# Fused Swin block and conv mixer: dilated convolutions spread over four column tiles, and VectorE's order rewritten

## The chip, the cores and the metric

One core of one Trainium2 chip runs the whole program. The metric is the device time of one execution in microseconds (us); lower is better. The kernel before was run three times: 1600.66, 1603.93 and 1605.35 us, median 1603.93. The engines are called PE (TensorE, matrix products), DVE (VectorE), ACT (ScalarE), POOL (GpSimd) and SP (SyncE, which issues the DMAs).

## The reference

Sixteen images of 128 channels and 32 x 32 pixels (1024 tokens), all float32, pass through two layers. The first is a Swin block (window attention over 8 x 8 windows with 8 heads, then an MLP of width 512); its output is the input of the second, a mixer of convolutions:

```python
out0 = gelu(conv1x1(x))
h_out, v_out = 3x3(7 taps, dilation 11, along w), 3x3(the same along h)   # depthwise
feats = [conv2d(out0, pyr_w[i], pyr_b[i], pad=(d, d), dil=(d, d), groups=dim // 4)
         for i, d in enumerate((1, 6, 12, 20))]      # 32 channels each: the pyramid
pyr = 3x3 depthwise(fuse_w * concat(feats) + fuse_b)
x_sca = |ifft2(conv1x1(x) * fft2(conv1x1(x)) * mask)| ...    # spectral branch
out = relu(x + c0*(1+edge)*h_out + c1*(1+edge)*v_out + c2*(1-0.3*edge)*pyr + c3*point + c4*x_sca)
return conv1x1(out)
```

The weights c0 to c4 come from a softmax over a small gate that reads the mean of out0; edge is the sigmoid of a 3x3 convolution to one channel.

## The kernel before

The work of two images is interleaved. `both(n, i, f, late)` exists once for each engine and is the body of a hardware loop: it runs the mixer of image n beside the attention and MLP of image i = n+1, the first norm and the q, k, v products of image f = n+2, and the end of the mixer of image late = n-1. It runs 15 times (n = 0 to 14, 13 of them in the loop); a setup and the attention of image 0 stand before it, and `conv_only(15)` behind it. Every engine executes its own list in the order in which it is written, and waits on semaphores.

**PE.** The head: scores(i,0), in_conv (1x1, line 652), scores(i,1), edge_products, then parts of the pyramid between gap_products (659) and mid_products (665), two tiny products whose answers DVE turns into the gate. Then eight slots j, one for each pair of windows: conv_early(j), scores(i,j+2) (line 530, which writes bank 2 and so waits for DVE to have read the scores before), prob_transposes(j), conv_late(j), values(i,j) (553, into banks 1 and 3 in turn). conv_early and conv_late are hand-placed pieces of the mixer: the spectral branch's transforms (dft_rows, r_even, ..., last_even), x2_conv, and parts of the pyramid in slots 0 and 1; out_conv(late) stands in slot 0. Behind the slots: last_odd, project, pyramid_conv(0) (683), n2_transposes(0) (481), pyramid_conv(1), n2_transposes(1), and mlp (593, 603), with the q, k, v products of image f inside it.

**The pyramid** (`pyramid(n, k, steps)`, line 693). Dilation d has a [128 x 32] weight for each of its nine taps and writes partitions 32d to 32d+31 of PSUM, that is, it runs in column tile d of PE. Half k (16 rows) has bank 4+k. A part runs over some of the nine taps, and in each over the dilations 3, 2, 1, 0; each matmul has only the rows and columns for which the shifted pixel lies in the image, so tile 0 (dilation 1) has nearly whole matmuls and tile 3 (dilation 20) small ones. In float32 each is two matmul instructions. Parts: half 0 in the head (taps 0-1, 2-5, 6-8), half 1 in slot 0 (0-3) and slot 1 (4-8). ACT copies each half to `pyr` (pyr_copy, 1578); SP stacks it with 12 DMAs into `pyr_stack` (stack_pyramid, 426), which pyramid_conv reads.

**DVE.** The head: gate_axes and add_magnitude of the late image, bias_max(i,0), gap, bias_max(i,1), attention_vectors, mixture(late), scaled_input, even_part, route_logits. bias_max(i,j) (1008) adds the bias (which frees bank 2), takes the row maximum and subtracts it. Slots: scale_values(j-1) (1022: reciprocal and product), bias_max(j+2), and pieces of the mixer (conv_slot, 1222). The 3x3 taps of h_out and v_out are 17 instructions over `hv` (1144), placed by `SLOT_TAPS`: one in slot 6, one behind norm2(i,0), two behind norm1_stats(f,1), the other 13 at the end. The next iteration's gate_axes follows the last tap.

**ACT** has the Gelus, exponentials and most copies from PSUM; first_tap (1562) in slot 2 starts hv; n2_copy(i,0) stands between square_odd and deviation2(i,1). **POOL** computes the dilated row and column convolutions (axis_conv) from the moment `act` is there.

Of the kernel before, what the change touches and what calls it, by code (L numbers as in the profile page):

```python
# [27 lines left out]
ALU = mybir.AluOpType  # L28
# [5 lines left out]
P = 128  # L34
# [13 lines left out]
GRID1 = S1 * S1  # L48
AXIS_DIL, AXIS_TAPS = 11, 7
# [5 lines left out]
def layout(*entries):  # L55
# [11 lines left out]
    ("fuse_w", 1), ("fuse_b", 1), ("pyr_b", 1), ("vis_b", 1),  # L67
# [72 lines left out]
def swin_conv_kernel(nc, x, cols, rows, mats, cons, rel_index, out):  # L140
    with ExitStack() as ctx:
# [33 lines left out]
        fuse_bias = sb("fuse_bias", 1)  # L175
        proj_shift = sb("proj_shift", P)
# [34 lines left out]
        hv, py = sb("hv", SIDE, SIDE), sb("py", SIDE, SIDE)  # L211
        pyr_stack = sb("pyr_stack", 4, GRID1)
# [110 lines left out]
        pyr_ps = sem("pyr_ps")  # L323
# [62 lines left out]
        SLOT_TAPS = (1, 1, 1, 1, 1, 1, 1, 2, 2, 3, 5)  # L386
# [3 lines left out]
        def _(sp):  # L390
# [35 lines left out]
            def stack_pyramid(n):  # L426
                sp.wait_ge(pyr_sb, 2 * n + 2)
                for s in range(3):
                    for j in range(4):
                        src = pyr[32 * j:32 * j + 32].rearrange("p h w -> p (h w)")  # L430
                        sp.dma_start(pyr_stack[32 * s:32 * s + 32, j, 0:33 * S1 + SIDE], src[:, s:s + 33 * S1 + SIDE])\
                          .then_inc(pyr_stacked, 16)
# [43 lines left out]
        def _(pe):  # L476
# [200 lines left out]
            def pyramid_conv(n, k):  # L677
                pe.wait_ge(pyr_stacked, 16 * 12 * n + 16 * 12)
# [10 lines left out]
            def inside(first, count, off):  # L689

                return max(first, -off), min(first + count, SIDE - off)

            def pyramid(n, k, steps):

                pe.wait_ge(act_sb, 2 * n + 2)
                grids = bank[4 + k].rearrange("p (h w) -> p h w", w=SIDE)
                for step in steps:
                    t = PYR_ORDER[step]
                    for d, dil in reversed(tuple(enumerate(DILS))):
                        dy, dx = (t // 3 - 1) * dil, (t % 3 - 1) * dil  # L700
                        (y0, y1), (x0, x1) = inside(16 * k, 16, dy), inside(0, SIDE, dx)
                        if y1 > y0:
                            last = pe.matmul(grids[32 * d:32 * d + 32, y0 - 16 * k:y1 - 16 * k, x0:x1], w_pyr[:, d, t],  # L703
                                             act[:, y0 + dy:y1 + dy, x0 + dx:x1 + dx],
                                             start=(step == 0), stop=(step == 8), skip_group_check=True)
                    if step == 8:
                        last.then_inc(pyr_ps, 1)
# [91 lines left out]
            def conv_early(n, j):  # L799

                if j == 1:
                    pyramid(n, 1, range(4, 9))
# [12 lines left out]
            def conv_late(n, j):  # L815
                if j == 0:
                    pyramid(n, 1, range(0, 4))
# [40 lines left out]
            def both(n, i, f, late):  # L858
# [28 lines left out]
                pyramid_conv(n, 0)  # L887
                n2_transposes(i, 0)
                pyramid_conv(n, 1)
# [87 lines left out]
        def _(dve):  # L977
# [201 lines left out]
            def mix_input(n):  # L1179

                dve.wait_ge(abs_sb, n + 1)
                dve.scalar_tensor_tensor(grid(xm[:]), act_in, mix[:, 3, 0:1], grid(xm[:]), ALU.mult, ALU.add)
                dve.drain()
# [38 lines left out]
            def conv_slot(n, j):  # L1222

                if j == 1:
                    sum_edge(n)
                    odd_part(n)
# [720 lines left out]
```

## Time and profile before

| | us |
|---|---|
| median of 3 runs (lowest, highest) | 1603.93 (1600.66, 1605.35) |
| the profiled execution | 1602.07 |
| its span, first to last instruction | 1600.2 |
| mean granted clock of PE | 0.974 of full speed |

The rows below come from one profiled execution. "L703" is line 703 of the kernel. A timeline row merges neighbouring instructions of one line; the bracket at its end is the time in which the engine stood idle before it, and who ended that. PEld are weight loads, which run beside the matmuls. Windows are given in us from the start of the span.

### The profile page before, as it was taken

Reading aid. Unit: us, or ns where it says so; the run is one execution under the profiler, and the core shown is the slowest. Engines: PE = TensorE matmul, PEld = TensorE weight load, DVE = VectorE, ACT = ScalarE, POOL = GpSimd, SP = SyncE. Lnnn points to the kernel's source line nnn. Section 1 sums busy time; section 2 is a strip of 40 time slices with the busy share of each in tenths; the row PEclk is TensorE's granted clock in tenths of the full one; section 3 lists DMA queues with packets and bytes.
Section 4 is the critical chain, followed back from the end, with each engine's and each line's share of the span. In section 5 each row is a group of like instructions: output and inputs, shape, how many; then the busy total and the mean of one; then the engine's idle time right before and its main releaser. Section 6 shows DMA issues by size and latency. Waiting matters only on the chain.

```text
span 1600.2 us, 36298 instructions
## 1 busy us (share of the span) xinstructions
PE 1453.8 (91%) x13904; PEld 843.6 (53%) x13904; DVE 1287.5 (80%) x2311; ACT 942.7 (59%) x1685; POOL 376.6 (24%) x315
## 2 busy tenths in 40 slices
PE   5699999998999999999999989999998999999884
PEld 3246556473654647465464745546464564646452
DVE  4728878888887888978788898878978787888857
ACT  3365747466484756748475574746657474664623
POOL 3022050502205040130504014050311405022040
PEclk9889999999999999999999999999999999999987
DMA  4012020120301112130111203012130201212020
GB/s 162 18 16 72 15 61 28 28 71 15 84 13 47 38 28 71 15 86 11 48 40 20 79 13 86 1 36 62 17 85 14 70 15 28 58 15 72 3 62 24
DMA packets 27904, 69.14 MB, mean 43 GB/s; under 512 B 12580, under 2 KB 12580, under 8 KB 27460
## 3 DMA queue, kind: packets, MB, share of 16 engines
q1 hardware_dynamic: 27844, 68.27, 17.0%
q8 instruction: 46, 0.75, 0.2%
q14 instruction: 14, 0.11, 0.0%
HBM read 22.41 MB, written 9.08 MB: 20 GB/s over the span
## 4 chain that ended last, share of the span: by engine, by line
DVE 39%; PE 28%; DVEq 16%; ACT 10%; issue 6%; DMA 1%; SPq 0%; ACTq 0%
DVE hv L1144 17%; PE bank L703 15%; ACT fft L1444 4%; DVEq L1015 4%; PE bank L530 3%; DVE row_max L1016 3%; DVEq L1027 3%; DVE stats L984 2%; PE bank L795 2%; ACT probT L1487 2%; DVEq L1039 2%; DVE score L1018 2%; DVEq L985 2%; DVE score L1013 1%; PE bank L673 1%
## 5 line engine op out<-in xcount | busy, mean ns | idle before, releaser
L703 PE MATMUL bank<-act,mats_sb 128*32 128x512 f32 (+11 forms) x2112 | 280.0, 492 | 0.0
L1144 DVE SCALAR_TENSOR_TENSOR hv<-ver,mix,hv 128x1024 f32<-128x1024 f32 x144 | 185.0, 1284 | 10.8
L1806 POOL TENSOR_TENSOR resT<-qC,proj_shift 128x1024 f32<-128x1024 f32 x16 | 38.0, 2377 | 622.6 <-DVE x1T L1036 618.0
L530 PE MATMUL bank<-k_heads,qC 128*64 128x512 f32 x512 | 143.0, 638 | 45.5 <-DVE score L1013 39.1
L703 PEld LDWEIGHTS bank<-act,mats_sb 128*32 128x32 f32 x2112 | 121.6, 113 | 104.7 <-issue 83.0
L1144 DVE SCALAR_TENSOR_TENSOR hv<-hor,mix,hv 128x1024 f32<-128x1024 f32 x128 | 164.4, 1284 | 10.6
L1444 ACT ACTIVATE fft<-bank 128x512 f32<-128x512 f32 x224 | 165.4, 810 | 12.8 <-PE bank L489 11.6
L489 PE MATMUL bank<-cons_sb,fft 128*128 128x128 f32 x1280 | 162.0, 280 | 7.8 <-DVE fft L1177 7.2
L1013 DVE TENSOR_TENSOR score<-bank,rel_bias 128x512 f32<-128x512 f32 x128 | 87.4, 682 | 96.9 <-PE bank L530 96.9
L1487 ACT ACTIVATE probT<-bank 128x512 f32<-128x512 f32 x128 | 77.7, 607 | 141.4 <-PE bank L541 139.9
L489 PEld LDWEIGHTS bank<-cons_sb,fft 128*128 128x128 f32 x1280 | 148.8, 192 | 20.8 <-DVE fft L1177 10.8
L1026 DVE RECIPROCAL inverse<-bank 128x128 f32<-128x128 f32 x128 | 122.0, 953 | 44.2 <-PE bank L557 44.2
L1482 ACT ACTIVATE score<-score 128x512 f32<-128x512 f32 x128 | 78.9, 628 | 129.5 <-DVE score L1018 129.3
L1826 POOL TENSOR_SCALAR hor<-act,cols_sb 128x1024 f32<-128x1024 f32 x16 | 30.4, 1902 | 486.4 <-ACT act L1521 417.7
L593 PE MATMUL bank<-nC,mats_sb 128*128 128x512 f32 x256 | 119.1, 599 | 0.0
L603 PE MATMUL bank<-fft,mats_sb 128*128 128x512 f32 x256 | 115.2, 592 | 0.0
L1836 POOL TENSOR_SCALAR axis_part<-act,cols_sb 128x320 f32<-128x320 f32 (+1 forms) x128 | 105.1, 821 | 21.6 <-issue 21.6
L1018 DVE TENSOR_TENSOR score<-score,row_max 128x512 f32<-128x512 f32 x128 | 98.8, 772 | 10.0 <-issue 0.5
L541 PEld LDWEIGHTS bank<-cons_sb,score 128*128 128x128 f32 x512 | 55.7, 142 | 79.1 <-issue 66.1
L1016 DVE TENSOR_REDUCE row_max<-score 128x8 f32<-128x512 f32 x128 | 87.8, 686 | 11.7
L1838 POOL TENSOR_TENSOR hor<-hor,axis_part 128x320 f32<-128x320 f32 (+1 forms) x64 | 94.3, 1473 | 9.4 <-issue 0.2
L683 PE MATMUL bank<-pyr_stack,mats_sb 96*32 96x512 f32 x768 | 88.9, 596 | 0.0
(181 smaller groups left out, 2642.1 us busy)
## 6 DMA issues: line engine op xcount, KB each, us to landing
pyr_stack<-pyr SPq DMA_DIRECT2D x192, 144.2 KB, 3.2
x_in<-x_dram SPq DMA_DIRECT2D x16, 512.0 KB, 4.6
k_heads<-kC SPq DMA_DIRECT2D x128, 64.0 KB, 2.3
edge<-edge_dram SPq DMA_DIRECT2D x16, 512.0 KB, 4.0
out_dram<-y_out SPq DMA_DIRECT2D x16, 512.0 KB, 2.6
k_heads<-rel_dram SPq DMA_DIRECT2D x2, 1024.0 KB, 13.2
mats_sb<-mats_dram SPq DMA_DIRECT2D x1, 1978.5 KB, 7.3
z_rows<-z_dram SPq DMA_DIRECT2D x48, 12.0 KB, 1.7
```

The costliest lines, as they stand in the source:

```text
L489: last = pe.matmul(dst[:, c * P:(c + 1) * P], src[:, at:at + P], rhs, start=True, stop=True)
L530: last = pe.matmul(bank[2][64 * e:64 * e + 64, :], qC[:, w * WT:(w + 1) * WT], k_heads[:, :, w], start=True, stop=True)
L593: pe.matmul(bank[b][:], w_up[:, f * P:(f + 1) * P], nC[:, HALF * k:HALF * k + HALF], start=True, stop=True).then_inc(up_ps, 1)
L603: last = pe.matmul(bank[b][:], w_down[:, f * P:(f + 1) * P], hidden[:, f, HALF * k:HALF * k + HALF], start=False, stop=(f == FC - 1))
L703: last = pe.matmul(grids[32 * d:32 * d + 32, y0 - 16 * k:y1 - 16 * k, x0:x1], w_pyr[:, d, t], act[:, y0 + dy:y1 + dy, x0 + dx:x1 + dx], st ...
L1016: dve.tensor_reduce(row_max[:, j % 3], score[:, j % 3], AX.X, ALU.max)
L1018: dve.tensor_tensor(score[:, j % 3], score[:, j % 3], row_max[:, j % 3].unsqueeze(2).broadcast_to([P, HEADS, WT]), ALU.subtract)\
L1026: dve.reciprocal(inverse[:, j % 2], ps[:, P:2 * P])
L1144: last = dve.scalar_tensor_tensor(hv[:], src, mix[:, a, k:k + 1], hv[:], ALU.mult, ALU.add)
L1444: return act_.activation(dst, src, ACT.Copy)
L1487: act_.activation(probT[:, j % 2].rearrange("p g t -> p (g t)"), bank[0][:], ACT.Copy)\
L1836: pool.tensor_scalar(axis_part[part], of, weight, 1.0, ALU.mult, ALU.mult)
```

## The change

`GIVEN = {0: (22, 3), 1: (28, 2)}`: rows 22 to 31 of dilation 1 are computed in column tile 3, and rows 28 to 31 of dilation 6 in column tile 2, both into bank 3. A planner in Python gives each tile its list of matmuls (low half, high half, given rows), always takes the next from the tile whose list is least far on (in columns), and cuts the result into five parts by time. The given rows have a copy of their own on ACT, a tile `pyr_given`, their own bias and weight columns, and split stack DMAs (18 for 12). Besides, orders change: on DVE bias_max(i,0) goes first, add_magnitude behind bias_max(i,1), bias_max(i,2), route_weights and odd_part ahead of slot 1, mix_input is split in two (slots 1 and 2), and the tap behind norm2(i,0) goes to slot 7; on PE both pyramid_conv stand before both n2_transposes; on ACT first_tap goes to slot 1 and n2_copy(i,0) behind normalise2(i,1).

```diff
+GIVEN = {0: (22, 3), 1: (28, 2)}
+        pyr_given = sb("pyr_given", SIDE - GIVEN[0][0] + 1, S1)
-        SLOT_TAPS = (1, 1, 1, 1, 1, 1, 1, 2, 2, 3, 5)
+        PYR_PARTS = (0, 0.12, 0.36, 0.58, 0.78, 1)
+        SLOT_TAPS = (1, 1, 1, 1, 1, 1, 1, 2, 3, 3, 5)
 SP, stack_pyramid
+                sp.wait_ge(given_sb, 2 * n + 2)
+                        if j not in GIVEN:
+                            sp.dma_start(pyr_stack[part, j, 0:end], own[:, s:s + end]).then_inc(pyr_stacked, 16)
+                            continue
+                        first, tile = GIVEN[j]
+                        low = (1 + first) * S1
+                        sp.dma_start(pyr_stack[part, j, 0:low - s], own[:, s:low]).then_inc(pyr_stacked, 16)
+                        sp.dma_start(pyr_stack[part, j, low - s:end], given[32 * tile:32 * tile + 32, 0:end - low + s])\
                           .then_inc(pyr_stacked, 16)
 PE
+            def pyramid_pieces():
+                ends = [GIVEN.get(d, (SIDE, d))[0] for d in range(4)]
+                chains = [[(d, 0, 16, t) for t in PYR_ORDER] + [(d, 16, ends[d], t) for t in PYR_ORDER] for d in range(4)]
+                for d, (first, tile) in GIVEN.items():
+                    chains[tile] += [(d, first, SIDE, t) for t in PYR_ORDER]
+                pieces, busy = [], [0, 0, 0, 0]
+                while any(chains):
+                    tile = min((g for g in range(4) if chains[g]), key=lambda g: busy[g])
+                    d, first, end, t = chains[tile].pop(0)
...
+                        busy[tile] += max(64, (y1 - y0) * (x1 - x0))
...
+            def pyramid(n, part):
                 pe.wait_ge(act_sb, 2 * n + 2)
+                pe.wait_ge(xm_sb, 2 * n + 2)
+                begin, until = (PYR_TIME * PYR_PARTS[part + k] for k in range(2))
+                for at, tile, d, first, t, y0, y1, x0, x1, low, final in PYR_PIECES:
...
+                    to = bank[4 if first == 0 else 5 if tile == d else 3].rearrange("p (h w) -> p h w", w=SIDE)
...
+                    if low:
+                        last.then_inc(pyr_low_ps, 1)
+                    elif final:
+                        last.then_inc(pyr_high_ps, 1)
 PE, both (slot 0: part 3; slot 1: part 4)
-                pyramid(n, 0, range(0, 2))
+                pyramid(n, 0)
                 gap_products(n)
-                pyramid(n, 0, range(2, 6))
+                pyramid(n, 1)
                 mid_products(n)
-                pyramid(n, 0, range(6, 9))
+                pyramid(n, 2)
...
+                    if j == 1:
+                        pe.wait_ge(given_sb, 2 * n + 2)
                     values(i, j)
...
                 pyramid_conv(n, 0)
+                pyramid_conv(n, 1)
                 n2_transposes(i, 0)
-                pyramid_conv(n, 1)
                 n2_transposes(i, 1)
 PE, conv_only
                 edge_products(n)
+                pyramid(n, 0)
                 gap_products(n)
-                pyramid(n, 0, range(0, 9))
+                pyramid(n, 1)
                 mid_products(n)
+                pyramid(n, 2)
 DVE, both
+                bias_max(i, 0)
                 if late is not None:
                     gate_axes(late)
-                    add_magnitude(late)
-                bias_max(i, 0)
                 gap(n)
                 bias_max(i, 1)
+                if late is not None:
+                    add_magnitude(late)
...
                 route_logits(n)
-                for j in range(PAIRS):
+                bias_max(i, 2)
+                route_weights(n)
+                odd_part(n)
+                for j in range(1, PAIRS):
                     if j in (4, 5):
                         conv_slot(n, j)
-                    if j > 0:
-                        scale_values(i, j - 1)
-                    if j == 3:
-                        conv_slot(n, j)
+                    scale_values(i, j - 1)
+                    if j == 1:
+                        mix_input(n)
+                    elif j == 3:
+                        r_even_bias(n)
                     if j + 2 < PAIRS:
                         bias_max(i, j + 2)
-                    if j < 3:
-                        conv_slot(n, j)
-                    if j == 0:
-                        route_weights(n)
+                    if j == 1:
+                        sum_edge(n)
+                    elif j == 2:
+                        mix_magnitudes(n)
                     taps(n, range(SLOT_TAPS[j], SLOT_TAPS[j + 1]))
 ACT (pyr_copy(n, 0) in slot 0 waits for pyr_low_ps, given_copy and pyr_copy(n, 1) in slot 1 for pyr_high_ps)
+            def given_copy(n):
+                act_.wait_ge(pyr_high_ps, 4 * n + 4)
+                for first, tile in GIVEN.values():
...
+                    act_.activation(pyr_given[part, 0:count, 1:1 + SIDE],
...
+                elif j == 1:
+                    first_tap(n)
...
                 if j == 1:
+                    given_copy(n)
                     pyr_copy(n, 1)
                     x2_copy(n)
                 elif j == 2:
                     spectrum_turn_copy(n)
-                    first_tap(n)
...
                 square_odd(n)
-                n2_copy(i, 0)
                 deviation2(i, 1)
                 normalise2(i, 1)
+                n2_copy(i, 0)
```

## Rows read from the trace of the kernel before

**Rows 1.** The page: busy time of each engine over the span.

```profile
PE 1453.8 (91%) x13904; PEld 843.6 (53%) x13904; DVE 1287.5 (80%) x2311; ACT 942.7 (59%) x1685; POOL 376.6 (24%) x315
```

**Rows 2.** Windows cut at line 652: us; busy PE, PEld, DVE, ACT, POOL; clock, DMA.

```profile
108.99:197.77 88.78, 86.41 (x860) 51.17 (x858) 73.77 (x138) 56.13 (x102) 20.94 (x19) 1.00 0.17 40
197.77:291.48 93.71, 88.25 (x864) 51.82 (x862) 77.59 (x143) 58.58 (x105) 23.27 (x19) 1.00 0.17 44
...
1330.89:1424.33 93.44, 88.21 (x864) 51.79 (x863) 77.47 (x143) 58.58 (x105) 23.24 (x19) 1.00 0.16 37
1424.33:1512.23 87.90, 81.64 (x772) 46.91 (x771) 73.34 (x122) 46.10 (x78) 20.21 (x18) 0.98 0.13 34
```

**Rows 3.** TensorE timeline, one iteration: start, us, instructions merged, [idle before <- releaser].

```profile
768.63 1.08 PE L530 MATMUL bank<-k_heads,qC 128*64 128x512 f32 x4 [2.87 <-DVE score L1013]
...
772.63 3.42 PE L703 MATMUL bank<-act,mats_sb 128*32 128x480 f32 x26
...
786.36 4.27 PE L703 MATMUL bank<-act,mats_sb 128*32 128x416 f32 x34
...
827.25 2.78 PE L683 MATMUL bank<-pyr_stack,mats_sb 96*32 96x512 f32 x24
...
834.53 0.66 PE L481 MATMUL bank<-cons_sb,nT 128*128 128x128 f32 x4 [1.18 <-ACT nT L1430]
...
857.22 1.98 PE L652 MATMUL bank<-xm,mats_sb 128*128 128x512 f32 x4
```

**Rows 4.** The page's groups of lines 530 and 683: busy, mean ns, idle before.

```profile
L530 PE MATMUL bank<-k_heads,qC 128*64 128x512 f32 x512 | 143.0, 638 | 45.5 <-DVE score L1013 39.1
...
L683 PE MATMUL bank<-pyr_stack,mats_sb 96*32 96x512 f32 x768 | 88.9, 596 | 0.0
```

**Rows 5.** VectorE timeline of the same iteration.

```profile
765.37 1.23 DVE L1204 SCALAR_TENSOR_TENSOR hv<-edge,hv 128x1024 f32<-128x1024 f32 x1 [0.20 <-issue]
...
767.89 0.68 DVE L1013 TENSOR_TENSOR score<-bank,rel_bias 128x512 f32<-128x512 f32 x1
...
770.25 0.68 DVE L1013 TENSOR_TENSOR score<-bank,rel_bias 128x512 f32<-128x512 f32 x1
...
772.81 0.22 DVE L1058 TENSOR_SCALAR vec<-bank,cols_sb 128x1 f32<-128x1 f32 x1 [0.32 <-PE bank L660]
...
774.61 1.42 DVE L1220 TENSOR_TENSOR hv<-hv,py 128x1024 f32<-128x1024 f32 x1
...
786.69 0.96 DVE L1026 RECIPROCAL inverse<-bank 128x128 f32<-128x128 f32 x1 [3.02 <-PE bank L557]
...
791.69 0.69 DVE L1013 TENSOR_TENSOR score<-bank,rel_bias 128x512 f32<-128x512 f32 x1 [3.67 <-PE bank L530]
...
824.12 0.96 DVE L1026 RECIPROCAL inverse<-bank 128x128 f32<-128x128 f32 x1 [0.87 <-PE bank L557]
```

**Rows 6.** An iteration with a clock fall (windows, VectorE); POOL's last instruction.

```profile
386.60:481.72 95.12, 89.87 (x865) 52.08 (x863) 81.28 (x143) 58.35 (x105) 22.69 (x19) 0.98 0.17 42
391.60:396.00 4.40, 4.40 (x20) 0.95 (x21) 3.47 (x6) 1.15 (x2) 3.77 (x5) 0.61 0.00 0
...
406.77 1.74 DVE L1018 TENSOR_TENSOR score<-score,row_max 128x512 f32<-128x512 f32 x1
...
789.47 0.82 POOL L1838 TENSOR_TENSOR ver<-ver,axis_part 128x320 f32<-128x320 f32 x1
```

**Rows 7.** ScalarE and SyncE timelines, slots 0 and 1.

```profile
780.16 0.77 ACT L1582 ACTIVATE pyr<-bank,fuse_bias,cols_sb 128x512 f32<-128x512 f32 x1
...
792.27 0.60 ACT L1487 ACTIVATE probT<-bank 128x512 f32<-128x512 f32 x1 [8.38 <-PE bank L541]
...
793.56 7.52 SPq L431 DMA_DIRECT2D pyr_stack<-pyr  x12
```

**Rows 8.** TensorE timeline of the last image.

```profile
1522.18 0.59 PE L659 MATMUL bank<-vec,mats_sb 128*128 128x1 f32 x2 [5.81 <-DVE vec L1051]
...
1522.77 10.53 PE L703 MATMUL bank<-act,mats_sb 128*32 128x512 f32 x63
```

More of the change, by code:

```diff
@@ L427, in stack_pyramid @@
                 sp.wait_ge(pyr_sb, 2 * n + 2)
+                sp.wait_ge(given_sb, 2 * n + 2)
+                flat = pyr.rearrange("p h w -> p (h w)")
+                given = pyr_given.rearrange("p h w -> p (h w)")
+                end = 33 * S1 + SIDE
                 for s in range(3):
+                    part = slice(32 * s, 32 * s + 32)
                     for j in range(4):
-                        src = pyr[32 * j:32 * j + 32].rearrange("p h w -> p (h w)")
-                        sp.dma_start(pyr_stack[32 * s:32 * s + 32, j, 0:33 * S1 + SIDE], src[:, s:s + 33 * S1 + SIDE])\
+                        own = flat[32 * j:32 * j + 32]
+                        if j not in GIVEN:
[5 more added lines that the diff above has]
+                        sp.dma_start(pyr_stack[part, j, low - s:end], given[32 * tile:32 * tile + 32, 0:end - low + s])\
                           .then_inc(pyr_stacked, 16)
@@ L687, in _, with inside @@
             PYR_ORDER = (4, 0, 1, 2, 5, 6, 7, 8, 3)
-            def inside(first, count, off):
-                return max(first, -off), min(first + count, SIDE - off)
-            def pyramid(n, k, steps):
-                pe.wait_ge(act_sb, 2 * n + 2)
[L696 to L707, printed above, removed]
+            def inside(first, end, off):
+                return max(first, -off), min(end, SIDE - off)
@@ new lines, in pyramid_pieces @@
+            def pyramid_pieces():
[7 more added lines that the diff above has]
+                    d, first, end, t = chains[tile].pop(0)
+                    (y0, y1) = inside(first, end, (t // 3 - 1) * DILS[d])
+                    (x0, x1) = inside(0, SIDE, (t % 3 - 1) * DILS[d])
+                    low = first == 0 and t == PYR_ORDER[8]
+                    if y1 > y0:
+                        pieces.append((busy[tile], tile, d, first, t, y0, y1, x0, x1, low, not chains[tile]))
+                        busy[tile] += max(64, (y1 - y0) * (x1 - x0))
+                    else:
+                        assert not low and chains[tile]
+                return pieces, max(busy)
@@ L801, in conv_early @@
                 if j == 1:
-                    pyramid(n, 1, range(4, 9))
+                    pyramid(n, 4)
                 elif j == 2:
@@ L816, in conv_late @@
                 if j == 0:
-                    pyramid(n, 1, range(0, 4))
+                    pyramid(n, 3)
                 elif j == 1:
@@ L1584, in pyr_copy @@
                                 scale=col("fuse_w")).then_inc(pyr_sb, 1)
+            def given_copy(n):
+                act_.wait_ge(pyr_high_ps, 4 * n + 4)
+                for first, tile in GIVEN.values():
+                    part, count = slice(32 * tile, 32 * tile + 32), SIDE - first
+                    act_.activation(pyr_given[part, 0:count, 1:1 + SIDE],
+                                    bank[3][part, 0:count * SIDE].rearrange("p (h w) -> p h w", w=SIDE), ACT.Identity,
+                                    bias=given_bias[part], scale=col("given_w")[part]).then_inc(given_sb, 1)
             def other_order(dst, k):
@@ L1902 @@
     put("pyr_b", conv["pyr_b"].reshape(-1))
+    for name, of in (("given_w", "fuse_w"), ("given_pyr_b", "pyr_b"), ("given_b", "fuse_b")):
+        for d, (_, tile) in GIVEN.items():
+            cols[32 * tile:32 * tile + 32, COLS[name][0]] = conv[of].reshape(-1)[32 * d:32 * d + 32]
     put("vis_b", np.repeat(conv["vis_b"], P))
```

34 lines of the change are left out of this document (25 added, 9 removed).

## The prediction

> **What bounds the kernel now.** The page's engine table comes first [rows 1]: PE is busy 91% of the span, DVE 80%, so either could set the time; what counts is who waits for whom inside one image. The window view cuts the run at each start of the 1x1 convolution (line 652) [rows 2]: 13 loop iterations lie between 197.77 and 1424.33, so one takes 94.35 us on average; undisturbed ones take 93.44. PE is busy 88.2 of these, so it has some 5 us of idle time, and the TensorE timeline of one iteration says where [rows 3]: 2.87 us before scores(i,1) and 1.18 us before the second turn of n2, the rest in pieces of half a microsecond. The page's group of line 530 gives the total of the first over the run: 39.1 us [rows 4]. Between 768.6 and 790.6 PE never waits; it is VectorE that waits for PE there, 3.02 and 3.67 us [rows 5]. After that DVE has hardly a gap up to its last tap, which ends when PE ends down() and in_conv. So PE holds the head, and both are tight in the rest: time returns to the span only if both give it.
>
> One more thing: in six of the 13 iterations the mean granted clock is under 1.00. In the one shown [rows 6] the granted clock is 0.61 in the 4.4 us behind the 2.88 us wait, a fall to the 1.2 GHz level, and that iteration takes 95.12 us.
>
> **The pyramid.** Its time is that of the fullest column tile. Dilation d has (96-2d)^2 columns over nine taps: 8836, 7056, 5184 and 3136. The old parts have 977, 1937, 1504, 2016 and 2402 columns in tile 0, and the rows give 3.42 us for 1937 and 4.27 for 2402 [rows 3]: about 1.75 ns a column, 15.5 us in all. Now rows 22 to 31 of dilation 1 (29 row-taps of 94 = 2726 columns) go to tile 3, and rows 28 to 31 of dilation 6 (8 x 84 = 672) to tile 2: 6110, 6384, 5856, 5862. The five parts are walled off from each other by full-array products, so each costs its own fullest tile; following the planner's list, these are 977, 1924, 1504, 1320 and 1152, together 6877. Saved: 1959 x 1.75 = **3.4 us** an image. 66 pieces become 81 (132 matmuls, 162): I take the count alone as free. Four tiles at once stream at nearly the same pace: line 683 puts 3 x 512 columns through each tile in 2.78 us [rows 3], 1.81 ns a column.
>
> **VectorE's head.** Today gate_axes and add_magnitude (2.52 us, from 765.37 to 767.89 [rows 5]) stand ahead of bias_max(i,0), whose first add frees bank 2 for scores(i,1). Now that add ends 0.7 us after the last tap, while in_conv ends 0.6 us after it: the 2.87 us wait shrinks to 0.1 or 0.2: **-2.7**. What is late next is mid_products. From the last tap's end DVE now does bias_max 2.3, gate 1.3, bias_max 2.3, add 1.2 and attention_vectors 1.8 us [rows 5]: 8.9 us. PE meanwhile ends in_conv at 0.6, scores at 1.6, edge at 2.5, part 0 at 4.1, the gap products at 4.5 and part 1 at 7.9 (1924 x 1.75 = 3.4), and waits 1.0 us: **+1.0**.
>
> **Slots.** bias_max(i,2) now precedes route_weights and odd_part; odd_part (1.2 us) and one half of mix_input move into the time in which DVE waited 3.02 and 3.67 us, and mix_magnitudes behind bias_max(4). The group behind 791.69 loses 1.2+1.3 us ahead of bias_max(4). So DVE follows PE's gain there, and PE keeps the lead; its half a microsecond of waiting for odd_product goes too: **-0.4**. ACT's pyr_copy(0) now waits for the low rows, which end some 1.1 us into part 3, and prob_copy(0) stands behind it; with 0.77 and 0.60 us [rows 7] this ends about with part 3 (1320 columns, 2.3 us): hidden, and under 0.2 if not. The new given_copy (two instructions, 320 and 128 columns a partition, where 512 take 0.77 [rows 7]: an estimate of 0.7 to 1.0 for both) stands ahead of pyr_copy(1), x2_copy and dft_rows: **+0.4** on PE. first_tap moves to slot 1, where ACT waits 8.38 us [rows 7]: nothing. Tap 2 (1.36 us) moves from between norm2(0) and residual_stats(1) to slot 7, beside DVE's waits of half a microsecond and 0.87 us [rows 5]: residual_stats(1), normalise2(1) and the n2 turns come 1.2 us earlier, and both pyramid_conv now stand before both turns: **-1.1**, of which **+0.3** is given back because up(4) then waits for the first gelu. The queue of SP gets six more stack issues: 12 take 7.52 us [rows 7], so 18 take 11.3, behind them widen_edge; pyramid_conv (827.25 [rows 3]) comes 33 us after the start of the stack, and the edge's first reader stands in slot 6, also far behind; both stay hidden. Without that cover they would cost 3.8 us. POOL's instructions are unchanged.
>
> **The shared cost of moving work under POOL.** POOL works up to 790.3 [rows 6]; DVE's moved instructions now fall into that time. The row to fear is a subtraction (line 1018) that takes 1.74 us there, where the others take about 0.7 [rows 6]. The Trainium skill, SBUF — State Buffer, "Who interferes with whom", says that a DVE instruction with two SBUF inputs and a GpSimd one that reads SBUF exclude each other for a whole instruction. The trace agrees (1.74 us); by the rule alone the term would be rival A's 2 us. Five such instructions stand between the last tap and mid_products, where each microsecond is PE's. Bounds: none, or two blocked at 1.05 us; I take **+0.6**. In the slots DVE has about 3 us of waits to absorb it.
>
> **Sum** for an iteration: -3.4-2.7-0.4-1.1+1.0+0.4+0.3+0.6 = -5.3 from 93.44, and the clock falls behind the vanished wait go, another -0.9 against the mean of 94.35: 88.15, so 6.2 x 13 = 81. The first iteration (88.78 [rows 2]) has no late image: 3.4+1.1 less 1 = 3.5. The last with attention (87.90): 5.3. The last image alone [rows 8]: part 0 fills the 5.81 us wait; mid_products comes after 1924 columns instead of 4418 (10.53 us for these, so 6 us earlier); parts 3 and 4 have 2472 columns instead of 4418 (3.4 us); not all reaches the taps, so 6. Together 81+3.5+5.3+6 = 96. The profiled execution took 1602.07 us (span 1600.2), 1.9 below the median of the runs: 1602.07-96 = 1506, median **1508**.
>
> **Rivals.**
> *A, the head is paid back* (chance 0.2): DVE, now the leader up to mid_products, loses 2 us more there to POOL, or PE's clock falls behind the new wait as it does behind the old one. For it: [rows 6]. Against: the waits are shorter. 1508+26 and a little at the ends: 1537.
> *B, the pieces run slower than their columns* (0.07): the pieces of 128 and 144 columns and the uneven ends of the five parts eat the 3.4 us; only the orders gain, 2.8 us an iteration and some 4 at the ends: 1563. For it: nothing in the rows shows so many small pieces in all four tiles.
> *C, slower* (0.04): the pieces of the new list no longer run four at a time. A tile's matmul that waits for its own tile holds up those of other tiles behind it; the old list went round the tiles in order, the new one doesn't. Two at a time, 24,212 columns take 24212 x 1.75/2 = 21.2 us, 5.7 more than today, and 9.1 more than the forecast's 12.0: 13 x (9.1-6.2) = 38 on the loop, less some 10 of slack: 1630. It decides from about 18 us a pyramid. Against: in the old list the tiles also differ threefold in columns, and still each part takes its fullest tile's time; and 24 matmuls of which one takes 592 ns (line 683 on the page) end in 2.78 us [rows 3, 4], five in flight at any time. The Trainium skill, TensorE: Matmul & The Clock Gate, "The mechanism", says that matmuls start and end strictly in program order; by that rule alone C would be the forecast, 1630. No view here shows the starts of single pieces, so the rule can't be weighed further than by the time of the parts, which is that of the fullest tile.
> *D, no difference* (0.02): DVE is the real bound. Against: its waits of 3.02 and 3.67 us.
>
> **Numbers.** Forecast 0.67. Its own range: without any collision and with a short copy on ACT, 7.1 us an iteration, 1495; with two blocked subtractions, 1525. The range reaches a little below, to 1492, and over A to 1542; B and C, 0.11 together, stay out. Some 0.3% (5 us) is what a measurement can tell from nothing. Faster: forecast, A, B: 0.94; the same 0.02; slower: C, 0.04.
>
> **What would show it.** Right: loop period 87.5 to 89; no wait before scores(i,1); about 1 us of waiting before mid_products; the pyramid's matmuls busy some 190 us in all (12.0 x 16) where they took 15.5 x 16; granted clock 1.00 in nearly all periods; n2's wait below 0.5. Wrong: a pyramid of 18 us or more (C); DVE two-input instructions above 1.5 us ahead of mid_products and waits of 3 us there (A); a wait before values(i,1) or dft_rows above 1.5 us, which would say that ACT's copies were mis-sized.

## The result and the profile after

The changed kernel takes 1527.12 us (median of four runs, 1520.09 to 1529.35), beside 1604.14 for the kernel before on the same chip: a ratio of 0.951, with an interval of 0.948 to 0.954. That is 77 us less; the forecast said 96 less, 1508. The time lies in the range, and 19 us of the gain are missing. The profiled execution took 1529.35 us, its span 1527.6.

The page of after: busy time [rows 1], the chain of work that ended last, and the groups that answer to [rows 4], with VectorE's first add of a softmax:

```profile
PE 1404.7 (92%) x14384; PEld 847.3 (55%) x14384; DVE 1321.4 (87%) x2312; ACT 955.9 (63%) x1717; POOL 408.7 (27%) x316
...
DVE 42%; DVEq 17%; PE 16%; ACT 15%; issue 8%; SPq 2%; DMA 1%; ACTq 0%
...
L743 PE MATMUL bank<-act,mats_sb 128*32 128x512 f32 (+16 forms) x2592 | 221.0, 430 | 0.0
...
L547 PE MATMUL bank<-k_heads,qC 128*64 128x512 f32 x512 | 142.0, 634 | 10.2 <-DMA k_heads<-kC 8.4
...
L1058 DVE TENSOR_TENSOR score<-bank,rel_bias 128x512 f32<-128x512 f32 x128 | 87.2, 681 | 50.4 <-PE bank L547 50.3
```

Two things catch the eye. The wait before the scores, 45.5 us with 39.1 of them behind DVE [rows 4], is down to 10.2, nearly all of it behind a DMA. And DVE, whose program has one instruction more, is busy 1321.4 us where it was 1287.5 [rows 1]: 34 us more for the same work. The chain says the same: PE's part of it is 16%, and was 28% before.

The windows of after, cut as in [rows 2] (this in_conv is line 669): the first three loop iterations, the sixth, and the whole loop.

```profile
198.27:289.44 91.17, 87.07 (x893) 52.72 (x894) 81.54 (x143) 59.32 (x107) 24.97 (x19) 0.98 0.19 45
289.44:381.34 91.90, 87.21 (x893) 52.30 (x894) 82.79 (x144) 59.37 (x107) 25.28 (x19) 0.98 0.18 45
381.34:469.04 87.70, 85.39 (x893) 51.72 (x894) 80.64 (x142) 59.18 (x107) 25.17 (x19) 1.00 0.19 47
...
647.68:736.07 88.39, 85.40 (x893) 51.72 (x894) 81.34 (x143) 59.18 (x107) 24.12 (x19) 1.00 0.19 46
...
198.27:1364.36 1166.09, 1118.81 (x11597) 677.13 (x11598) 1063.61 (x1847) 770.23 (x1391) 322.92 (x247) 0.99 0.18 45
```

The last row divided by 13 is the mean iteration: 89.70 us, against 94.35 before and 88.15 forecast. The same row of the kernel before, for the 13 iterations from 197.77 to 1424.33:

```profile
197.77:1424.33 1226.56, 1158.21 (x11208) 675.40 (x11207) 1031.10 (x1847) 759.92 (x1365) 297.87 (x247) 0.99 0.17 42
```

This pair is the best tool of this study. The first number is the loop's time, the second what PE works in it, and their difference the time in which PE stands still: 68.4 us before, 47.3 after. So the loop's gain of 60.5 us is 39.4 of work and 21.1 of waiting. The forecast's 81 were 56 of work (3.4 for the pyramid and 0.9 for the clock falls, times 13) and 25 of waiting. **The waiting came almost as forecast; 16.5 of the 20 missing microseconds are PE's own busy time.**

Outside the loop: the setup came out 2.8 us longer (a start of in_conv at 111.75 where it was 108.99), the first iteration 2.3 shorter (86.52), the last one with attention 4.1 (83.84), the last image 8.6 (79.40). With the loop's 60.5 that makes 72.6, as the two spans differ.

The TensorE timeline of one iteration of after [rows 3]:

```profile
649.48 1.08 PE L547 MATMUL bank<-k_heads,qC 128*64 128x512 f32 x4
...
653.48 3.36 PE L743 MATMUL bank<-act,mats_sb 128*32 128x480 f32 x35
656.79 0.38 PE L682 MATMUL bank<-vec,mats_sb 128*128 128x1 f32 x2
...
663.37 2.41 PE L743 MATMUL bank<-act,mats_sb 128*32 128x320 f32 x36
665.84 0.43 PE L570 MATMUL bank<-probT,v_pair 128*32 128x64 f32 x16
...
666.31 2.14 PE L743 MATMUL bank<-act,mats_sb 128*32 128x186 f32 x38
...
673.13 2.05 PE L506 MATMUL bank<-cons_sb,fft 128*128 128x128 f32 x16 [0.64 <-ACT fft L1502]
...
678.56 1.09 PE L498 MATMUL bank<-cons_sb,fft 128*128 128x128 f32 x8 [1.79 <-ACT fft L1502]
...
711.98 1.46 PE L498 MATMUL bank<-cons_sb,nT 128*128 128x128 f32 x8
```

No bracket stands behind scores(i,1) (649.48) and none behind n2 (711.98), where 2.87 and 1.18 us stood. Two new waits have come: 0.64 before dft_rows, 1.79 before turn_spectrum. And the same places on VectorE [rows 5]:

```profile
656.83 2.11 DVE L1268 TENSOR_TENSOR hv<-hv,py 128x1024 f32<-128x1024 f32 x1
...
659.85 2.33 DVE L1129 TENSOR_TENSOR fft<-xs 128x465 f32<-128x465 f32 x1
...
668.41 1.50 DVE L1130 TENSOR_TENSOR fft<-xs 128x15 f32<-128x15 f32 x1
...
671.26 2.33 DVE L1227 SCALAR_TENSOR_TENSOR xm<-act,mix,xm 128x1024 f32<-128x1024 f32 x1
673.51 0.68 DVE L1058 TENSOR_TENSOR score<-bank,rel_bias 128x512 f32<-128x512 f32 x1
```

A subtraction of 15 columns takes 1.50 us here, and 0.17 elsewhere. In the stretch between the gap products and scores(i,3) DVE had 8 us of rest before; it has 1 now. The windows of the stretch, before and then after:

```profile
772.25:790.56 18.31, 18.31 (x163) 9.59 (x163) 10.35 (x29) 6.23 (x11) 16.13 (x14) 1.00 0.09 32
```

```profile
653.10:668.38 15.28, 15.22 (x186) 9.22 (x185) 14.24 (x29) 6.92 (x12) 13.62 (x12) 1.00 0.07 17
```

From the list of PE's waits of after: us in total, how many times, and the longest:

```profile
PE bank L498 <- ACT fft L1502: 16.0, 12, 1.8
PE bank L682 <- DVE vec L1112: 14.2, 10, 2.1
...
PE bank L498 <- ACT nT L1488: 12.3, 14, 5.7
...
PE bank L506 <- ACT fft L1502: 10.1, 16, 0.6
```

The first two are means of two kinds of iteration. Five of the 13 wait 2.13 us before mid_products (line 682) and at most 0.45 before turn_spectrum (line 498, behind fft); six others wait 1.76 to 1.79 us before turn_spectrum and at most 0.52 before mid_products.

### The profile page after: what moved, and what is told of

Same layout as the page of the kernel before. It is cut to its first block, busy times and chain, and to the rows that moved or that the text cites. A ratio compares the mean times of both kernels' runs of the same rounds, so it can differ in the third digit from the quotient of the medians.

```text
span 1527.6 us, 37499 instructions
## 1 busy us (share of the span) xinstructions
PE 1404.7 (92%) x14384; PEld 847.3 (55%) x14384; DVE 1321.4 (87%) x2312; ACT 955.9 (63%) x1717; POOL 408.7 (27%) x316
## 4 chain that ended last, share of the span: by engine, by line
DVE 42%; DVEq 17%; PE 16%; ACT 15%; issue 8%; SPq 2%; DMA 1%; ACTq 0%
DVE hv L1189 15%; ACT fft L1502 6%; DVEq L1060 5%; DVE row_max L1061 4%; PE bank L743 4%; DVEq L1072 3%; DVE score L1063 3%; PE bank L547 2%; DVE inverse L1071 2%; PE bank L610 2%; ACT nT L1488 2%; ACT probT L1545 2%; ACT fft L1662 2%; DVEq L1106 2%; DVE score L1058 1%
## 5 line engine op out<-in xcount | busy, mean ns | idle before, releaser
L743 PE MATMUL bank<-act,mats_sb 128*32 128x512 f32 (+16 forms) x2592 | 221.0, 430 | 0.0
L506 PE MATMUL bank<-cons_sb,fft 128*128 128x128 f32 x1280 | 161.1, 279 | 11.3 <-ACT fft L1502 10.1
L1895 POOL TENSOR_SCALAR hor<-act,cols_sb 128x1024 f32<-128x1024 f32 x16 | 25.0, 1565 | 488.3 <-ACT act L1579 426.3
L743 PEld LDWEIGHTS bank<-act,mats_sb 128*32 128x32 f32 x2592 | 125.5, 111 | 50.5 <-issue 30.2
L547 PE MATMUL bank<-k_heads,qC 128*64 128x512 f32 x512 | 142.0, 634 | 10.2 <-DMA k_heads<-kC 8.4
L1905 POOL TENSOR_SCALAR axis_part<-act,cols_sb 128x320 f32<-128x320 f32 (+1 forms) x128 | 139.9, 1093 | 21.6 <-issue 21.6
L1071 DVE RECIPROCAL inverse<-bank 128x128 f32<-128x128 f32 x128 | 121.5, 950 | 10.2 <-PE bank L574 8.7
L610 PE MATMUL bank<-nC,mats_sb 128*128 128x512 f32 x256 | 122.9, 608 | 0.0
L1063 DVE TENSOR_TENSOR score<-score,row_max 128x512 f32<-128x512 f32 x128 | 95.1, 743 | 9.6
L1061 DVE TENSOR_REDUCE row_max<-score 128x8 f32<-128x512 f32 x128 | 87.8, 686 | 11.7
L1554 ACT ACTIVATE fft<-bank,fold_b 128x512 f32<-128x512 f32 x128 | 80.7, 684 | 10.4 <-PE bank L610 10.4
```

Of the source, the lines that this page charges most:

```text
L506: last = pe.matmul(dst[:, c * P:(c + 1) * P], src[:, at:at + P], rhs, start=True, stop=True)
L547: last = pe.matmul(bank[2][64 * e:64 * e + 64, :], qC[:, w * WT:(w + 1) * WT], k_heads[:, :, w], start=True, stop=True)
L610: pe.matmul(bank[b][:], w_up[:, f * P:(f + 1) * P], nC[:, HALF * k:HALF * k + HALF], start=True, stop=True).then_inc(up_ps, 1)
L743: last = pe.matmul(to, w_pyr[:, d, t], act[:, y0 + dy:y1 + dy, x0 + dx:x1 + dx], start=(t == 4), stop=(t == PYR_ORDER[8]), skip_group_chec ...
L1061: dve.tensor_reduce(row_max[:, j % 3], score[:, j % 3], AX.X, ALU.max)
L1063: dve.tensor_tensor(score[:, j % 3], score[:, j % 3], row_max[:, j % 3].unsqueeze(2).broadcast_to([P, HEADS, WT]), ALU.subtract)\
```

## The experiments

Theory after the result: DVE now leads, and what is missing is what POOL takes from it. Rivals: ACT's copies set the pace in the slots; the pyramid's term is smaller; PE still leads. The kernels were measured in three groups, each beside its own runs of the kernel before (1605.17, 1603.39 and 1600.92 us), so kernels of different groups are compared by their ratios to it; 0.001 is 1.6 us. Ratios to hold them against: 1 before, 0.951 after.

### The two halves of the change

**pyramid_alone** has the new piece list, its copies and DMAs, with every order as before; **orders_alone** the reverse.

In pyramid_alone VectorE's head reads, against the changed kernel (the slots, SLOT_TAPS, first_tap and the n2 turns go back likewise):

```diff
-                bias_max(i, 0)
                 if late is not None:
                     gate_axes(late)
+                    add_magnitude(late)
+                bias_max(i, 0)
                 gap(n)
                 bias_max(i, 1)
-                if late is not None:
-                    add_magnitude(late)
```

> The new pyramid with its copies and DMAs, every order of VectorE, ScalarE and the n2 turns as before. If the pyramid's fullest tile is all that counts, 3.4 us for each of 15 iterations and some 6 at the end come back: 1548 to 1555. If part of it is lost because the wait before scores(i,1) stays and the new copies delay dft_rows, about 2.5 us an iteration: 1560 to 1565.

> The old pyramid with every order of the changed kernel. The wait before scores(i,1) (2.9 us) and the second n2 turn (1.2 us) go: if nothing takes their place 1604 - 15 x 3.5 = 1552. If the shared port of VectorE and GpSimd gives back what the moved instructions gain, 1570 to 1580; the slots' waits of VectorE for the pyramid (3.0 and 3.7 us) are still there to absorb blocked instructions, so I take 1560.

Measured: pyramid_alone 1553.87 us, 0.969 [0.9655, 0.973], 51 less; orders_alone 1573.62, 0.980 [0.9775, 0.982], 32 less. Together 83, and both at once gave 77 to 78: nearly a sum. pyramid_alone came as expected; orders_alone missed its 1560 by 14 us and lies in the range given there for a shared port that takes the gain back. The loop of each, pyramid_alone first:

```profile
197.66:1386.51 1188.85, 1118.89 (x11597) 674.43 (x11598) 1043.90 (x1847) 770.19 (x1391) 290.55 (x247) 0.99 0.18 44
```

```profile
196.52:1401.48 1204.96, 1165.11 (x11208) 680.46 (x11206) 1064.16 (x1847) 761.68 (x1366) 322.99 (x247) 0.99 0.18 42
```

The pyramid brings all of its loop gain as PE work (1158.2 to 1118.9) and leaves PE's waiting where it was (70.0); the orders take the waiting from 68.4 to 39.9 and give 7 back as busy time. DVE's busy time rises with the orders, to 1064.2, and by 13 with the pyramid alone. In orders_alone the wait before mid_products is 29.1 us over the run (14 times, up to 2.1), double that of after: it is made by the orders, not by the shorter pyramid.

The undisturbed iterations (granted clock 1.00) of the two say more of PE's own work, which is 88.2 us in the kernel before and 85.4 in after: it is 85.0 in pyramid_alone (931.90 to 1021.36) and 88.5 in orders_alone (288.38 to 379.94). So the new pyramid takes 3.2 of the 3.4 us away, and the orders add 0.3 to 0.4 of busy time with the same matmuls.

### POOL taken away

**after_less_pool** and **before_less_pool** run only the first instruction of each of POOL's two dilated convolutions: of their 18 instructions an image 16 are left out (the page's count of POOL goes from x316 to x60; the expectation's "18 of 20" miscounts), and the dilated taps with them. The signal that the convolution is done moves to that first instruction; no wait of PE, DVE or ACT in either full kernel ends with POOL, so that this signal comes sooner can't be what is measured.

```diff
                 for off in offsets:
+                    if off != 0:
+                        continue
```

> The changed kernel, GpSimd's row and column convolutions cut to their first instruction each (18 of 20 instructions an image left out). Theory T (GpSimd's instructions block VectorE's two-input ones for some 5 us an image, and VectorE leads through the head and slots 0 and 1): VectorE busy falls from 82 to about 77 us a period, the period from 89.7 to about 87, the time to 1485 to 1495. Rival R (PE waits for ScalarE's copies, whose order is at fault): no change, 1520 to 1530.

> The kernel before, GpSimd's convolutions cut to their first instruction each, as in after_less_pool. If the blocked time before was harmless (VectorE waited 3.0 and 3.7 us for PE right behind it), little: 1590 to 1602. If the changed kernel's loss of 27 us had been there all along, 1575 to 1580, and the shared port would be no reason why the change fell short.

Measured: after_less_pool 1500.23 us, 0.935 [0.933, 0.937], 26 to 27 below after, though short of the 1485 to 1495 expected. before_less_pool 1602.97, 0.9998 [0.9983, 1.0014]: nothing. The busy times of after_less_pool, and of before_less_pool:

```profile
PE 1393.9 (93%) x14384; PEld 841.1 (56%) x14384; DVE 1238.5 (83%) x2312; ACT 956.9 (64%) x1717; POOL 101.2 (7%) x60
```

```profile
PE 1451.0 (91%) x13904; PEld 842.2 (53%) x13904; DVE 1239.0 (78%) x2311; ACT 944.5 (59%) x1685; POOL 100.0 (6%) x59
```

With POOL cut short, DVE's work is the same in both kernels, 1239 us. So what was left out of POOL had lengthened DVE's instructions by 48.5 us in the kernel before (1287.5 less 1239.0), which cost nothing, and by 82.9 in the changed one (1321.4 less 1238.5), which cost 27. What it cost PE is in the waits view of after_less_pool:

```profile
PE bank L682 <- DVE vec L1112: 5.4, 9, 0.9
...
PE bank L498 <- ACT fft L1502: 1.5, 2, 1.1
```

14.2 and 16.0 have become 5.4 and 1.5 us, and the loop:

```profile
194.57:1337.88 1143.31, 1111.80 (x11598) 672.80 (x11596) 993.15 (x1847) 771.27 (x1391) 71.54 (x39) 1.00 0.19 46
```

The mean clock is 1.00, and PE is busy 7.0 us less than in after with the same matmuls: the clock falls are gone too. An iteration takes 87.95 us.

### Who leads

**after_less_tap** leaves out one of DVE's 13 last taps (t = 12); **after_less_pe** leaves out one of the three weight rows of pyramid_conv, some 1.8 us of PE an image; **exponent_later** leaves nothing out and moves ACT's exponent(i,3) behind the spectrum's copies.

In this order the edits are:

```diff
-                taps(n, range(SLOT_TAPS[PAIRS + 2], 18))
+                taps(n, [t for t in range(SLOT_TAPS[PAIRS + 2], 18) if t != 12])
```

```diff
-                for y in range(3):
+                for y in (0, 2):
```

```diff
+                    if j == 2:
+                        exponent(i, 3)
...
-                    if j + 2 < PAIRS:
+                    if j + 2 < PAIRS and j != 1:
                         exponent(i, j + 2)
```

> The changed kernel with one of VectorE's 13 taps at the end of an iteration left out (1.36 us of VectorE, nothing else). Theory T (VectorE leads): most of 14 x 1.36 = 19 us, 1508 to 1515. If PE leads: under 5 us, 1522 to 1528.

> The changed kernel with one of three rows of weights left out of each pyramid_conv (1.8 us of PE an iteration, nothing else). If PE leads: up to 15 x 1.8 = 27 us less, 1500. Theory T: part of it at most, 1515 to 1527, since the n2 turns and the MLP start sooner but the taps end when they did.

> The changed kernel, ScalarE's exponent(i,3) moved behind the row spectrum's copies and prob_copy(i,2) in slot 2, so that the copies no longer wait for VectorE. Rival R: the 1.8 us wait of PE before turn_spectrum goes and the time with it: 1500 to 1505. Theory T: the wait goes, VectorE leads and nothing moves: 1524 to 1530.

Measured: after_less_tap 1512.52, 0.942 [0.940, 0.945], some 14 us less for 15 taps of 1.3 us; after_less_pe 1530.05, 0.954 [0.952, 0.957], nothing gained; exponent_later 1527.04, 0.952 [0.950, 0.954], nothing, but not for the reason expected, since the wait did not go. The loop of after_less_pe:

```profile
199.71:1364.49 1164.78, 1093.71 (x11389) 669.68 (x11388) 1063.74 (x1846) 769.73 (x1391) 316.28 (x247) 0.99 0.18 45
```

PE works 25 us less and waits 24 us more (71.1 against 47.3), and the loop's time stays: DVE leads behind pyramid_conv, up to the last tap. That PE led the head before is shown by pyramid_alone, where 39.3 us less of PE's work made the loop 37.7 us shorter, and by before_less_pool, where 48.5 us less of DVE gave nothing. Why exponent_later did nothing for the wait before turn_spectrum (21.1 us there) is in its ScalarE timeline:

```profile
583.42 0.32 ACT L1609 ACTIVATE edge_rows<-edge_sum,half_vis_b 32x32 f32<-32x32 f32 x1 [2.80 <-DVE edge_sum L1175]
583.64 1.87 ACT L1502 ACTIVATE fft<-bank 128x512 f32<-128x512 f32 x2
```

The tanh of the edge stands ahead of the same copies, and it waits for sum_edge, which DVE does behind bias_max(i,3). With exponent(i,3) out of the way, this wait came next, behind the same DVE work. So this kernel does not test the rival of ACT's copies. attention_ver, below, does: ACT's order is that of after there, and the wait before turn_spectrum is gone.

### Moving work out of POOL's time

Five kernels that leave nothing out. **odd_mix_back** puts odd_part and mix_input back behind bias_max(3), as before the change. **ver_later** makes POOL wait for xm_mixed ahead of its column convolution. **attention_first** puts attention_vectors ahead of add_magnitude(late); **attention_ver** is both of the last two, **attention_ver_exp** also exponent_later.

The edits of odd_mix_back, ver_later and attention_first:

```diff
-                odd_part(n)
...
-                    if j == 1:
-                        mix_input(n)
...
+                        odd_part(n)
+                        mix_input(n)
```

```diff
                 axis_conv(n, 0, OFFSETS[2:])
+                pool.wait_ge(xm_mixed, n + 1)
                 axis_conv(n, 1, OFFSETS[:3])
```

```diff
+                attention_vectors(n)
                 if late is not None:
                     add_magnitude(late)
-                attention_vectors(n)
```

> The changed kernel, GpSimd's column convolution held back until VectorE has done mix_magnitudes (one wait on xm_mixed; the column taps read it 40 us later). Nothing is left out. Theory T: odd_part and mix_input of slots 0 and 1 are no longer blocked (about 3 us), VectorE meets GpSimd in slots 2 to 4 with few two-input instructions: 1.5 us an iteration, 1505. Rival R: 1527. If the blocked time only moves along: 1520 to 1527.

> The changed kernel with odd_part and the first half of mix_input back behind bias_max(i,3). By the prediction they fill time in which VectorE waited, so that this costs 1.2+1.3 us an iteration: 1560. By theory T VectorE leads there and only the blocked part of them differs: they leave GpSimd's time, lose up to 2.5 us of blocking and delay nothing: 1520 to 1530.

> The changed kernel with attention_vectors ahead of add_magnitude(late), so that mid_products no longer waits for it (1.3 us, 1.7 where it is blocked); VectorE's work up to mixture is the same. If the wait before mid_products (39.6 us in all) and the clock falls behind it matter: it shrinks by half, no or one fall in the loop, 1 to 1.5 us an iteration, 1505 to 1513. Theory T alone (VectorE leads from there on whatever PE does): 1522 to 1528.

> attention_first with the held-back column convolution of ver_later. If the two prices hide each other (a blocked VectorE behind mid_products, a late mid_products ahead of it), both together give what neither gives alone: 1495 to 1505. If not, as attention_first.

> attention_ver with exponent(i,3) moved as in exponent_later. If PE leads again once VectorE is freed, ScalarE's order is worth up to 1 us an iteration more: 1485 to 1495. If VectorE still leads: as attention_ver within 3 us.

Measured, with the DVE busy time of the page beside it:

| kernel | us | ratio, interval | DVE busy | loop |
|---|---|---|---|---|
| after | 1527.12 | 0.951 [0.948, 0.954] | 1321.4 | 1166.09 |
| ver_later | 1526.63 | 0.951 [0.949, 0.953] | 1295.1 | 1167.88 |
| odd_mix_back | 1518.31 | 0.948 [0.946, 0.950] | 1298.7 | 1160.38 |
| attention_first | 1518.58 | 0.947 [0.945, 0.950] | 1322.4 | 1160.15 |
| attention_ver | 1511.03 | 0.944 [0.942, 0.946] | 1293.2 | 1151.02 |
| attention_ver_exp | 1510.13 | 0.943 [0.941, 0.945] | 1293.6 | 1151.42 |

By ratio, odd_mix_back and attention_first gain about 6 us each on after (each interval touches that of after; the two loops say 5.7 and 5.9), attention_ver 11, the last 13. The last two can't be told apart, and both are clearly faster than either kernel of the study. Against what was expected, ver_later (1505) and attention_ver (1495 to 1505) gained less, attention_first came between its two ranges, and odd_mix_back did better than both the prediction's 1560 and the theory's 1520 to 1530. ver_later shows that DVE's lost time is not a price by itself: 26 us less of it, and no gain, because PE's waits only changed places. From its list of PE's waits:

```profile
PE bank L682 <- DVE vec L1112: 13.2, 11, 2.1
PE bank L498 <- ACT nT L1488: 12.5, 18, 5.5
...
PE bank L506 <- DVE fft L1222: 10.7, 15, 0.7
```

The wait before turn_spectrum is 1.5 us there, but the odd product (L1222) is late again, and mid_products as late as ever. attention_first does the opposite: its wait before mid_products is no longer in the list, that before turn_spectrum is 27.9 us. Only both together free PE at both places: attention_ver's list has no wait before mid_products and 1.5 us before turn_spectrum. The loop of attention_ver:

```profile
196.96:1347.98 1151.02, 1112.98 (x11597) 672.93 (x11596) 1037.09 (x1847) 771.17 (x1391) 312.73 (x247) 1.00 0.19 46
```

## Why the prediction was right, and where it was short

**The pyramid, -3.4.** Right in mechanism: the five parts take their fullest tile's time. Part 1 takes 3.36 us for 1924 columns (1.75 ns each), part 3 2.41 for 1320, part 4 2.14 for 1152; the group of line 743 is busy 221.0 us where line 703 was 280.0, 3.7 an image. In the loop, though, PE's busy time fell by 2.8 only, from 88.2 to 85.4 in undisturbed iterations. The stretch from the gap products to scores(i,3), which holds parts 1 to 4, went from 18.31 to 15.28, 3.0. The step that failed is that the parts are "walled off from each other by full-array products, so each costs its own fullest tile": between parts 3 and 4 stand the products of values(i,0), which are column-tiled themselves (128*32), and in the kernel before they ran beside the end of part 3:

```profile
782.57 3.17 PE L703 MATMUL bank<-act,mats_sb 128*32 128x512 f32 x30
785.18 0.30 PE L553 MATMUL bank<-probT,v_pair 128*32 128x64 f32 x2
785.38 0.51 PE L703 MATMUL bank<-act,mats_sb 128*32 128x416 f32 x1
...
785.58 0.58 PE L703 MATMUL bank<-act,mats_sb 128*32 128x496 f32 x1
```

The products of line 553 started 1.0 us before the last piece of part 3 had ended (785.18, and 785.58 + 0.58), it seems in tiles whose pieces were done. Behind the balanced part 3 they start at 665.84, when its last piece has ended (663.37 + 2.41). From the start of part 3 to that of part 4 there were 3.79 us, 0.26 more than its 2016 columns at 1.75 ns; now there are 2.94, 0.63 more than its 1320 columns. That is the 0.4 us that are missing in this stretch. The other 0.2 lie elsewhere and are not the pyramid's: PE's busy time rose by 0.3 with the orders alone. Together 0.6 us an iteration, 8 us in all. The sign that the prediction named, some 190 us for the pyramid's matmuls, did not come (221.0), but it was mis-sized on both sides: its 15.5 x 16 would be 248 where line 703 has 280.0.

**The wait before scores(i,1), -2.7.** Right: 39.1 us became 1.6 (the one of line 547 behind the score), 2.3 an image.

**The wait before mid_products, +1.0, and the shared cost, +0.6.** 14.2 us over 16 images, 0.9 each, where 1.6 were forecast for both. With POOL cut short 5.4 are left, 0.3 each. So collisions there cost about 0.6 as said. DVE's chain is as long as said, too, 9.0 us from the last tap's end to that of attention_vectors in the iteration at 647.68; it is PE that comes later, since in_conv ends 1.8 us behind the last tap there, not 0.6. The mean hides that the wait is 2.13 us or nearly nothing; that its mean came near the forecast is in part luck.

**The slots, -0.4, with DVE's "3 us of waits to absorb it".** This failed. The cover was measured on a kernel whose slow pyramid had made it; the change took it away. odd_part and mix_input, moved early, take 1.50 and 2.33 us for single instructions (0.17 and 1.27 elsewhere), bias_max(i,3) comes late, behind it sum_edge and then ACT's copies: 16.0 us before turn_spectrum where 1.5 stood, 0.9 an image that no term held. Against it, the odd products (lines 1177 and 1170 of before, 7.8 us of PE's waits) are on time, 0.5 an image. odd_mix_back undoes these two moves alone: the 16.0 us go down to 1.6, the wait for the odd product (L1222) comes back with 4.6, and the loop is 5.7 us shorter. So the two moves were a loss in this kernel, as far as intervals that touch can say. The Trainium skill, SBUF — State Buffer, "Who interferes with whom", says that a DVE instruction with two SBUF inputs contends with a GpSimd one that reads SBUF. The trace agrees: a 15-column instruction of two SBUF inputs takes 1.50 us beside POOL, and the 16 mix_input instructions take 33.3 us where they take 20.4 with POOL cut short. Not all of the 83 us is of that kind: TENSOR_SCALAR instructions, which read one tensor and a column of scalars, have 17.6 of it.

**The clock falls, -0.9.** Failed, and the largest item. PE's busy time above 13 undisturbed iterations is 11.2 us before (1158.2 less 13 x 88.23) and still 8.1 after (1118.8 less 13 x 85.44): 0.2 an iteration instead of 0.9. Six of 13 iterations had a fall before and five have one now, so the prediction's 1.00 "in nearly all periods" did not come. The falls came with the new waits. In the iteration at 198.27:

```profile
209.56 0.38 PE L682 MATMUL bank<-vec,mats_sb 128*128 128x1 f32 x2 [2.13 <-DVE vec L1112]
```

```profile
210.18:214.54 4.36, 4.36 (x31) 2.56 (x32) 4.13 (x12) 1.25 (x2) 4.04 (x3) 0.61 0.02 6
```

Behind the new wait of 2.13 us the granted clock is 0.61 for 4.4 us, on the 1.2 GHz level for most of it, as behind the old one [rows 6], and the iteration takes 91.17 us. Three of the five falls stand in iterations with this wait; the other two (915.75 and 1274.37) wait 0.4 us or less before mid_products, and there the clock falls behind the wait of 1.8 us before turn_spectrum (in the first of them the wait ends at 946.64, and the granted clock is 0.53 from 948 to 951 us). Not every such wait has its fall: two of the five iterations that wait 2.13 us run at 1.00. With POOL cut short, where the wait before mid_products is never longer than 0.9, and in attention_ver, where it is gone and that before turn_spectrum is never above 1.1, each of the 13 iterations runs at 1.00. This was rival A's second half, "PE's clock falls behind the new wait", to which, with its first half, the prediction gave a chance of 0.2. What came is A in part: POOL takes 22.8 us of the loop (1166.1 less 1143.3), 7.8 of which the forecast held, so 15 of A's 26 us.

**ACT's copies, +0.4.** dft_rows waits 0.64, 16 times: 10.1 us. The exponent's place alone was not the cause of the slots' loss. **SP's queue:** its 18 issues take from 672.62 to 684.33, 11.7 us where 11.3 were said, and no row shows a reader waiting for the stack. **n2, -1.1 + 0.3:** the bracket of 1.18 us is gone; PE's waits for ACT's nT are 12.3 us where they were 27.2, 0.9 an image.

**The last image, 6.** It gained 8.6. Its gap products now wait 4.01 us instead of 5.81:

```profile
1457.87 0.58 PE L676 MATMUL bank<-vec,mats_sb 128*128 128x1 f32 x2 [4.01 <-DVE vec L1096]
...
1458.45 5.53 PE L743 MATMUL bank<-act,mats_sb 128*32 128x480 f32 x35
```

**The sum.** The mean iteration of 89.70 us lies outside the 87.5 to 89 that the prediction named as its sign. Missing in the loop against the forecast: PE's work at full clock 0.6, the clock falls 0.7 and PE's waiting 0.3 an iteration, 1.55 in all or 20 us; outside it, the setup's 2.8 against, the last image's 2.6 for. after_less_pool, 1500, is what the forecast gives without its +0.6 (1508 less 8); the agreement hides an overlap of the pyramid that was missed and waits that came out shorter than said.

**The rivals.** B asked for 1563 and a pyramid without gain: the parts rule it out. C asked for 21.2 us a pyramid: the parts 1 to 4 take 10.6 us together. (Its matmul of line 683 takes 596 ns by the page, not 592, which changes nothing.) The rule under TensorE: Matmul & The Clock Gate, "The mechanism", of the Trainium skill, that matmuls start and end strictly in program order, read as C read it, would have made the kernel slower; the parts show that pieces of four tiles still run side by side in the new order. And the rows of line 553 above do show single starts, which the prediction thought no view would: two of its products start at 785.18, before two matmuls of line 703, at 785.38 and 785.58, that stand ahead of them in the program. The page's rule would have them the other way round; by the starts that the trace shows, strict program order does not hold here across column tiles. D asked for no difference; DVE is the bound now, though not before.

Open: what part of the 2.8 us in the setup belongs to the change (after_less_pool reaches this in_conv at 109.3 us, attention_ver at 110.4 and after_less_tap at 111.5, all with after's setup, so that a part of it is spread between executions); and which single instruction gives way when DVE and POOL meet, since it changes from iteration to iteration.

## What to carry to other kernels

When a change makes the engine faster that gave others their cover, price again what stood under that cover: here 48.5 us of DVE time lost to POOL were free, and 82.9 us cost 27. Put instructions with two SBUF inputs where POOL rests, and feed a tiny product that gates the rest first. Two kernels that each leave out one instruction of one engine say who leads at that place, and one row, loop time with PE's busy time in it, says what kind of time a change took away.

## What was unexpected of the hardware

When a wait of PE is moved, clock falls can turn up behind the new one, even where it is only 1.8 us long, and a fall costs 1.5 to 1.8 us of busy time (86.89 to 87.21 us in iterations with one, 85.44 without). Matmuls of one column tile start before matmuls of another that stand ahead of them in the program. And POOL stretched DVE's whole program by 4% (48.5 of 1239 us) without anything of it showing in the time while PE led (0.9998 with POOL cut short), by 7% once DVE did.
